# A decoder layer on one core: in each state-space chunk y's return stands one step earlier, the normalisation later, with a shorter Newton step

## The reference

```python
xz = x @ W_in.T;  x_ssm, z = split(xz)                 # state-space part, 512 channels, 16 states
x_ssm = silu(conv4(x_ssm) + conv_b)                    # causal, per channel
B, C, d = x_ssm @ W_x.T;  dt = softplus(d * W_dt + b_dt)
h[t] = exp(dt[t] * A) * h[t-1] + (x_ssm[t] * dt[t]) * B[t]
y[t] = sum_n h[t, :, n] * C[t, n] + x_ssm[t] * D
x = layernorm(x + (y * silu(z)) @ W_out.T)
x = layernorm(x + cross_attention(x, ctx))             # 16 heads, 154 context tokens
x = layernorm(x + moe(x))                              # 4 experts, the 2 best, weighted; moe adds its own x
```

## Time and profile before

| | us |
|---|---|
| median of 3 timed runs (1684.32 to 1684.8) | 1684.76 |
| the profiled execution | 1675.18 |
| its span | 1673.4 |
| granted TensorE clock, mean | 0.919 of full |

### The profile page before, as it was taken

How to read it: one execution, slowest core, us unless ns; L and a number is a source line. 1 busy time by engine, 2 the same in 40 slices (tenths; PEclk the granted TensorE clock), 3 DMA queues, 4 the chain that set the end, 5 groups by cost and what they waited for, 6 DMA issues and landing times. The chain is left out here.

```text
span 1673.4 us, 22601 instructions
## 1 busy us (share of the span) xinstructions
PE 1335.8 (80%) x7484; PEld 930.7 (56%) x7484; DVE 1465.3 (88%) x2698; ACT 1114.0 (67%) x2452; POOL 915.1 (55%) x663
## 2 busy tenths in 40 slices
PE   7687778788777877787886969988988898887880
PEld 5566556666656666565665644446445644462460
DVE  5999999999999999999999966697869786978578
ACT  5867887788788778878877524337633763375570
POOL 1778878877887788788778701102710271027015
PEclk9889899989989898998898989999999999999895
DMA  7201210220122022102102012100010000000000
GB/s 234 67 14 45 70 58 13 70 70 32 40 70 71 1 70 70 50 21 70 64 1 89 14 38 103 36 1 1 26 55 1 1 26 26 1 1 1 25 1 25
DMA packets 37927, 69.87 MB, mean 42 GB/s; under 512 B 3569, under 2 KB 31570, under 8 KB 33586
## 3 DMA queue, kind: packets, MB, share of 16 engines
q1 hardware_dynamic: 37810, 68.43, 12.0%
HBM read 59.77 MB, written 8.65 MB: 41 GB/s over the span
## 5 line engine op out<-in xcount | busy, mean ns | idle before, releaser
L900 POOL TENSOR_TENSOR state_c<-state,c_area 128x1024 f32<-128x1024 f32 x256 | 602.0, 2362 | 167.8 <-DVE state L970 148.9
L970 DVE TENSOR_TENSOR_SCAN state<-decay,ps 128x512 f32<-128x512 f32 x512 | 620.6, 1212 | 0.0
L686 ACT ACTIVATE decay<-step_area,negA 128x255 f32<-128x255 f32 x1024 | 432.6, 496 | 0.4 <-DVE step_area L1049 0.4
L945 DVE TENSOR_TENSOR ps<-step_area,ps 128x512 f32<-128x512 f32 x512 | 349.7, 683 | 8.0 <-PE ps L368 6.2
L384 PE MATMUL ps<-ident_sb,state_c 128*128 128x128 f32 x2048 | 293.3, 291 | 12.9 <-POOL state_c L900 11.9
L1578 POOL TENSOR_TENSOR big<-big,g_sb 128x1024 f32<-128x1024 f32 x29 | 79.4, 2739 | 406.6 <-ACT big L1467 404.9
L384 PEld LDWEIGHTS ps<-ident_sb,state_c 128*128 128x128 f32 x2048 | 253.5, 151 | 39.0 <-POOL state_c L900 21.5
L368 PE MATMUL ps<-parts,sel_bc_sb 96*128 96x256 bf16 x256 | 74.7, 292 | 102.7 <-DVE ps L961 80.2
L1391 PE MATMUL ps<-w_sb,weights 128*128 128x512 f32 x256 | 122.6, 615 | 0.0
L1426 PE MATMUL ps<-w_sb,hT 128*128 128x256 f32 x512 | 120.0, 388 | 2.4 <-ACT hT L1536 1.9
L1666 DVE BATCH_NORM_STATS2 stats<-big 128x6 f32<-128x256 f32 x256 | 88.4, 413 | 30.4 <-ACT big L1541 21.1
(11 more groups left out here) (211 smaller groups left out, 2357.9 us busy)
## 6 DMA issues: line engine op xcount, KB each, us to landing
c_area<-c_scratch SPq DMA_DIRECT2D x32, 1024.0 KB, 6.5
weights<-in_xT SPq DMA_DIRECT2D x16, 256.0 KB, 3.1
res<-in_x SPq DMA_DIRECT2D x16, 256.0 KB, 2.8
x_scratch<-res SPq DMA_DIRECT2D x16, 256.0 KB, 8.1
weights<-x_scratch SPq DMA_DIRECT2D x4, 1024.0 KB, 8.1
xa<-x_scratch SPq DMA_DIRECT2D x4, 1024.0 KB, 5.6
out_x<-acc SPq DMA_DIRECT2D x4, 1024.0 KB, 4.4
w_sb<-in_w SPq DMA_DIRECT2D x2, 1024.0 KB, 13.0
```

Source lines behind the costliest of these rows:

```text
L686: nc.scalar.activation(decay[:, n % RING, j, 1:], dt_sb[:, i[1] % 2, j, 1:], ACT.Exp, scale=negA[:, j * NS + n:j * NS + n + 1]).then_inc(s ...
L900: nc.gpsimd.tensor_tensor(state_c[:, n % RING, :, :], state[:, n % RING, :, :], c_bc[:, q, n, :].unsqueeze(1).to_broadcast([P, CT, TC]), A ...
L945: nc.vector.tensor_tensor(bu_ps[m % 3][:, :].rearrange("p (j n) -> p j n", j=2), u_sb[:, i[1] % 2, 2 * h:2 * h + 2, :], b_ps[n % 2][:, 0:T ...
L970: nc.vector.tensor_tensor_scan(state[:, n % RING, pair, :].rearrange("p j n -> p (j n)"), decay[:, n % RING, pair, :].rearrange("p j n -> ...
```

## The change

- PE (`turn`): `y_back`, `y_back`, `out_tile`, `out_tile` stand at steps 10, 11, 12 and 13 in every chunk; before it was 11 to 14, and 10 to 13 in the last alone.
- ACT: the copies of y stand at 13 and 14, the first sum at 15 of the same chunk, the second at step 0 of the next; the Silus at 9, not 10; `spreads` at 5, `guess` at 8, `normalise` at 13, where it is first in the list, ahead of `next_lead` and the first copy. `take_keys(0)` comes first in its list, and in the last chunk the keys', context's and queries' entries stand ahead of the others of the same step.
- GpSimd: `centre` stands at step 14 of the chunk in which the sums are taken, `variance` at 3, `newton` at 6.
- `variance` is one tensor_scalar operation (multiply, add) in place of two tensor_tensor ones, Newton's halving and subtraction likewise one; with `variance`'s that makes a step of six counted operations (`s_nw`), not seven. `centre` becomes a tensor_scalar. The constants' tile `coef` and its five fills are gone.

```diff
@@ PE, turn
                 if finish:
-                    early_by = 0 if prepare else 1
-                    work += [(11 - early_by, lambda: y_back(last, 0)), (12 - early_by, lambda: y_back(last, 1)),
-                             (13 - early_by, lambda: out_tile(last, 0)), (14 - early_by, lambda: out_tile(last, 1))]
+                    work += [(10, lambda: y_back(last, 0)), (11, lambda: y_back(last, 1)),
+                             (12, lambda: out_tile(last, 0)), (13, lambda: out_tile(last, 1))]
@@ ACT, turn
                 if settle:
-                    work += [(0, lambda: take_sum(old, 0)), (1, lambda: take_sum(old, 1)), (3, lambda: spreads(old)), (6, lambda: guess(old)),
-                             (9, lambda: normalise(old))]
+                    work += [(0, lambda: take_sum(old, 1)), (5, lambda: spreads(old)), (8, lambda: guess(old)),
+                             (13, lambda: normalise(old))]
                 if prepare:
                     work += [(3, lambda: take_xi(k, 0)), (4, lambda: take_xi(k, 1)), (5, lambda: take_conv(k, 0)), (7, lambda: take_conv(k, 1)), (8, lambda: take_z(k, 0)),
-                             (9, lambda: take_z(k, 1)), (10, lambda: silus(k)), (11, lambda: copies(k)),
+                             (9, lambda: take_z(k, 1)), (9, lambda: silus(k)), (11, lambda: copies(k)),
                              (12, lambda: terms(k, 0)), (12, lambda: terms(k, 1)), (12, lambda: terms(k, 2)),
                              (12, lambda: terms(k, 3)), (12, lambda: softplus(k)),
                              (13, lambda: next_lead(k))]
                 if finish:
-                    work += [(14, lambda: take_y_back(last, 0)), (15, lambda: take_y_back(last, 1))]
+                    work += [(13, lambda: take_y_back(last, 0)), (14, lambda: take_y_back(last, 1)), (15, lambda: take_sum(last, 0))]
                 if prepare:
                     work.append((15, lambda: first_decay(k)))
                 if i[1] == NCH - 2:
-                    work.append((13, lambda: take_keys(0)))
+                    work.insert(0, (13, lambda: take_keys(0)))
                 if i[1] == NCH - 1:
-                    work += [(4, lambda: take_keys(1)), ...
+                    early = [(4, lambda: take_keys(1)), ...
+                    work = early + work
@@ ACT, behind the turns
-            for t in range(CTT):
-                take_sum(shift(last, -1), t)
+            take_sum(shift(last, -1), 1)
@@ GpSimd, variance, centre, newton
-                nc.gpsimd.tensor_tensor(var[:, :], spread[:, :], per_dm, ALU.mult).then_inc(s_mv, 1)
-                pool.wait_ge(s_mv, at(k, 2, 2))
-                nc.gpsimd.tensor_tensor(var[:, :], var[:, :], eps, ALU.add).then_inc(s_nw, 1)
+                nc.gpsimd.tensor_scalar(var[:, :], spread[:, :], 1.0 / DM, LN_EPS, ALU.mult, ALU.add).then_inc(s_nw, 1)
-                nc.gpsimd.tensor_tensor(mean[:, :], total[:, :], minus_per_dm, ALU.mult).then_inc(s_mv, 1)
+                nc.gpsimd.tensor_scalar(mean[:, :], total[:, :], -1.0 / DM, None, ALU.mult).then_inc(s_mv, 1)
-                nc.gpsimd.tensor_tensor(newt[:, :], newt[:, :], half, ALU.mult).then_inc(s_nw, 1)
-                pool.wait_ge(s_nw, at(k, 7, 4))
-                nc.gpsimd.tensor_tensor(newt[:, :], one_half, newt[:, :], ALU.subtract).then_inc(s_nw, 1)
+                nc.gpsimd.tensor_scalar(newt[:, :], newt[:, :], -0.5, 1.5, ALU.mult, ALU.add).then_inc(s_nw, 1)
@@ GpSimd, turn
                 if settle:
-                    work += [(0, lambda: centre(old)), (2, lambda: variance(old)), (4, lambda: newton(old))]
+                    work += [(3, lambda: variance(old)), (6, lambda: newton(old))]
...
+                if finish:
+                    work.append((14, lambda: centre(shift(i, -1))))
```

More of the change, by code:

```diff
@@ L103, in mamba_block @@
         shift_sb = sb("shift_sb", [P, CTT])
-        coef = sb("coef", [P, 5, CTT])
         b_ps = [ps[:, k, :] for k in range(2)]
@@ L130, in mamba_block @@
         s_par = sem("s_par")
-        s_coef = sem("s_coef")
         s_in = sem("s_in")
@@ L653, in spreads @@
             def spreads(k):
-                act.wait_ge(s_mv, at(k, 2, 1))
+                act.wait_ge(s_mv, at(k, 1, 1))
                 for t in range(CTT):
@@ L662, in normalise @@
             def normalise(k):
-                act.wait_ge(s_nw, at(k, 7, 7))
+                act.wait_ge(s_nw, at(k, 6, 6))
                 for t in range(CTT):
@@ L670, in guess @@
             def guess(k):
-                act.wait_ge(s_nw, at(k, 7, 1))
+                act.wait_ge(s_nw, at(k, 6, 1))
                 nc.scalar.activation(lnv[:, :], var[:, :], ACT.Ln).then_inc(s_ln, 1)
@@ L749, in turn @@
                 if i[1] == NCH - 2:
-                    work.append((13, lambda: take_keys(0)))
+                    work.insert(0, (13, lambda: take_keys(0)))
                 if i[1] == NCH - 1:
-                    work += [(4, lambda: take_keys(1)), (5, lambda: take_context(0)), (6, lambda: take_context(1)),
+                    early = [(4, lambda: take_keys(1)), (5, lambda: take_context(0)), (6, lambda: take_context(1)),
                              (6, lambda: take_context(2)), (7, lambda: take_context(3)), (7, lambda: take_values(False)),
                              (8, lambda: take_values(True))]
-                    work += [(9 + v, lambda v=v: take_query(v)) for v in range(G + 1)]
-                    work += [(15, lambda: spare_keys())]
+                    early += [(9 + v, lambda v=v: take_query(v)) for v in range(G + 1)]
+                    early += [(15, lambda: spare_keys())]
+                    work = early + work
                 for n in range(NS):
@@ L868, in newton @@
                 nc.gpsimd.tensor_tensor(newt[:, :], rstd[:, :], rstd[:, :], ALU.mult).then_inc(s_nw, 1)
-                pool.wait_ge(s_nw, at(k, 7, 2))
+                pool.wait_ge(s_nw, at(k, 6, 2))
                 nc.gpsimd.tensor_tensor(newt[:, :], newt[:, :], var[:, :], ALU.mult).then_inc(s_nw, 1)
-                pool.wait_ge(s_nw, at(k, 7, 3))
-                nc.gpsimd.tensor_tensor(newt[:, :], newt[:, :], half, ALU.mult).then_inc(s_nw, 1)
-                pool.wait_ge(s_nw, at(k, 7, 4))
-                nc.gpsimd.tensor_tensor(newt[:, :], one_half, newt[:, :], ALU.subtract).then_inc(s_nw, 1)
-                pool.wait_ge(s_nw, at(k, 7, 5))
+                pool.wait_ge(s_nw, at(k, 6, 3))
+                nc.gpsimd.tensor_scalar(newt[:, :], newt[:, :], -0.5, 1.5, ALU.mult, ALU.add).then_inc(s_nw, 1)
+                pool.wait_ge(s_nw, at(k, 6, 4))
                 nc.gpsimd.tensor_tensor(rstd[:, :], rstd[:, :], newt[:, :], ALU.mult).then_inc(s_nw, 1)
-                pool.wait_ge(s_nw, at(k, 7, 6))
+                pool.wait_ge(s_nw, at(k, 6, 5))
                 nc.gpsimd.tensor_tensor(shift_sb[:, :], mean[:, :], rstd[:, :], ALU.mult).then_inc(s_nw, 1)
@@ L907, in _ @@
             nc.gpsimd.memset(decay[:, :, :, 0], 0.0).then_inc(s_zero, 1)
-            for c, value in enumerate((0.5, 1.5, 1.0 / DM, LN_EPS, -1.0 / DM)):
-                nc.gpsimd.memset(coef[:, c, :], value).then_inc(s_coef, 1)
-            half, one_half, per_dm, eps, minus_per_dm = (coef[:, c, :] for c in range(5))
             pool.sem_inc(s_sum, RING)
@@ L913, in _ @@
             nc.gpsimd.memset(ones[:, :], 1.0).then_inc(s_ones, 1)
-            pool.wait_ge(s_coef, 5)
             first, last = (None, 0), (None, NCH - 1)
@@ L920, in _ @@
             for k in (shift(last, -1), last):
-                centre(k)
+                if k == last:
+                    centre(k)
                 variance(k)
```

## The result

The changed kernel takes 1698.2 us (median of 4 runs, 1697.07 to 1699.82); the kernel before, in 4 runs beside it, 1684.54 (1682.09 to 1684.8). The ratio is 1.0085, with a 95% interval of 1.0068 to 1.0103: slower, 2.8 us under the 1701 forecast. The profiled execution took 1699.82 us (span 1698.0, clock 0.919), 24.6 more than the profiled one of before. Of the two differences, 13.7 timed and 24.6 profiled, the larger one rests on a single reading of before, and the smaller on four; the first experiment shows how far such readings scatter. One later run of before, 1754.45 us at a granted clock of 0.799, is left out of every ratio.

The account below looks back on a forecast made before the run. VectorE, busy 892.1 of 900 us in the chunks, was taken as the bound. New idle 22.9 us (twelve chunks x 1.5, plus 2.2, 2.2, 0.5) less 6.3 gives +16.6 on the 1684.76 median: 1701.4 us, range 1684 to 1717.

Parts of the forecast that it names:

- the 1701 forecast: Whole kernel: net +16.6 us added to the timed median of 1684.76 gives 1701.4 us; chance 0.72.
- The mechanism: Chunk ends: second transposition ahead of row 14, output tile ahead of row 15; PE waits for y's copy, rows come late.
- X: Price of an ordinary chunk in VectorE idle time near rows 14 and 15: 1.5 us, taken between 0.1 and 2.95.
- The half-clock end: Upper end of X: all PE work from transposition to row 15 at half clock, row 15 2.95 us late.
- The full-clock end: Lower end of X: all at full clock, second copy sets the output tile's start, row 15 0.1 us late.
- a share of 2.2 for five chunks: Extra 2.2 us in all for chunks 4, 8, 12 (no VectorE carry additions) and those after 4 and 12 (ACT late).
- Chunk 14: `keys(0)` and `y_back` share PE's step 10; transposition waits for ACT's two key copies, row 13 2.2 us late.
- Chunk 1: Has no `normalise`; cost 0 to 1.4 us, taken as 0.5.
- The last chunk: Key copies no longer behind the mean and a pair of squares; two row-product stalls go, gain 2.4 us (0 to 2.7).
- The sum: VectorE idle time: 22.9 us new, 6.3 off (boundary and last-chunk waits), net +16.6 us.
- Faster: Rival: VectorE's waits go and none comes, with y's copy at 653 instead of 655; 1679.6 us, chance 0.13.
- Half clock throughout: Rival: every ordinary chunk (2 to 13) pays 2.95 us, last chunk's 2.4 not gained; +37, 1722 us, chance 0.06.

Follow-up runs that it names:

- the first experiment: The kernel before, unchanged, profiled a second time: 1678.44 us, 3.3 more than its first profiled run.
- the first two edits: PE's four steps put back in the changed kernel: 1673.74 us, ratio to before 0.9951; PE's steps alone moved in the kernel before: 1722.61 us, 1.0236.
- the eight zero products: Changed kernel plus eight PE products with a tile of zeros, added into y's bank ahead of the second transposition's wait: 1683.04 us, ratio to before 0.9994.
- `normalise` last: Changed kernel with ACT's `normalise(old)` still at step 13 but last in the list, behind the first copy of y: 1683.77 us, ratio to before 1.0002.
- the two experiments before the last: Kernel before with only ACT's copies and first sum moved, keys first: 1698.14 us; PE's-steps-back kernel with Silus at 10, `normalise` at 9: 1713.11 us.

## Why the prediction was right, and where it was not

*The mechanism was right.* PE's steps carry the loss, as the first two edits show; it comes through what is queued behind the second transposition, and through the clock. The copy of y was to come 1.2 us earlier against row 14: it starts 1.81 us ahead of it (669.63, 671.44) where it was 0.56: 1.25, of which 0.1 is row 14's own delay (against row 13's product it is 1.15). PE's wait: "about 4", 4.02. The idle time ahead of `make_bu` is 28.7 us where 25 were named, and ACT's waits for GpSimd's mean are gone. The two waits a chunk came in chunks 3, 4, 8 and 12 alone: at row 14 the others wait 0.2 us or less, where I had 0.35. The clock was to fall ahead of the transposition; it does so in the odd chunks 3 to 13 and in 14, and just behind its start in the other ones from 2 to 12. I hadn't thought of that case, and in the ordinary chunks it is the cheap one.

*X, the price of an ordinary chunk*, was 1.5 between 0.1 and 2.95. It is no number in between but two: 0.8 to 1.05 in chunks 2, 6 and 10, where the clock comes back inside the output product well before its end, and 1.9 to 2.1 in 5, 7, 9, 11 and 13, where it is at half nearly to the end (chunk 3, where the copy is 0.9 us later than in these, has 2.67). That 1.5 lies between the two is why the middle served; the average of these eight is 1.6. The half-clock end was 0.9 too high: between transposition and row 15's multiplication I had 7.6 us, chunk 11 shows 6.83 (729.42 to 736.25), most of it because I doubled the full rate of output tile and input to 4.3, which took 3.70. The full-clock end, 0.1, agrees with the eight zero products, where these rows wait nowhere. The Trainium skill ("TensorE: Matmul & The Clock Gate", "HAM oscillation — how this bites in real kernels") has each pass with a long wait restart at the low clock; the trace agrees in that chunks 2 to 14 all have such a stretch around their wait of 3.2 to 4.0 us, and differs in chunk 1, where the clock stays at full through 3.04 us. By it alone X was to be near 2.95; measured is 0.8 to 2.1.

*Chunks 4, 8 and 12 were mis-sized.* I had them at 1.5 plus a share of 2.2 for five chunks, 1.9; they cost 2.4 each. ACT's copy is there no earlier against VectorE than before, 3.1 us behind row 13's product. The cause stands at the start of the chunk, PE, after, then before:

```profile
512.82 1.39 PE L382 MATMUL ps<-ident_sb,state_c 128*128 128x128 f32 x8 [1.95 <-DVE yg L924]
514.01 5.04 PE L303 MATMUL ps<-weights 128*128 128x256 f32 x16
```

```profile
503.29 3.62 PE L305 MATMUL ps<-weights 128*128 128x256 f32 x16
```

With PE's steps back, in the same chunk:

```profile
501.79 3.62 PE L303 MATMUL ps<-weights 128*128 128x256 f32 x16
```

PE waits for VectorE's gating of y, its clock falls, and the convolution takes 5.04 us instead of 3.62; ACT waits for it 5.59 us and is late up to the copy. I had looked for low-clock stretches only around the copy of y. With PE's four steps back and all else as in after, the convolution stays at full clock in this chunk and the copy stands 1.8 us behind row 13's product in all three, so the lateness comes with PE's early steps. By what way is open: with the eight products of zeros the copy is late in chunks 4 and 8 (3.1 and 2.8 us) and not in 12 (1.8), with `normalise` last in 12 alone (2.1, against 0.8).

*Chunk 14*: 2.58 us at row 13, forecast 2.2, by the mechanism named; it went away with the one step given back. *Chunk 1*: nothing at rows 14 and 15, forecast 0.5. *The last chunk* gained 0.9 us, forecast 2.4: rows 6 and 7 still wait 0.93 each where the earlier trace rows has 1.81 and 0.93. The sum was +16.6 on VectorE's idle time and the trace shows +20.7: +2.3 in chunks 2 to 13, +0.4 in 14, +1.5 in the last; the rest are small ones both ways. That this gave 1701 against 1698 is partly luck, two misses that offset: between the profiled executions the time grew by 24.6 us, 8.0 more than the sum, and the median to which I added the sum lay 9.6 above the profiled time of before.

*The gain was in the sum, its cause was not.* The sum takes 6.3 us off, waits at chunk boundaries and in the last chunk. With PE's steps back the rest of the change gives 0.4 to 0.5%, 6 to 8 us, and the idle time falls from 8.0 (11.2 in the second execution) to 4.5 us. But I had set down ACT's waits for GpSimd's mean as ACT's idle time alone. Behind them PE waits too, at `in_proj`; the waits view of before and of the kernel with PE's steps back:

```profile
PE ps L288 <- ACT weights L586: 29.7, 14, 2.9
```

```profile
PE ps L286 <- ACT weights L584: 5.2, 4, 1.7
```

In such a wait PE's clock can fall and a row come late, as row 5 did in the first experiment; over 30 to 930 us half clock is on for 126 us against 181. I read ACT's idle time for its length, not for what PE does meanwhile. That the gain comes by this way fits these figures, but no run takes the waits for the mean away alone; taken in pieces, the change without its PE part turns into a loss (the two experiments before the last).

*The rivals.* "Faster" needed the copy of y 2 us earlier than I counted; one microsecond more brings no difference (`normalise` last). "Half clock throughout" is nearly what chunks 5, 7, 9, 11 and 13 do, at 1.9 to 2.1 us and not 2.95. That PE's steps alone in the kernel before took 1722.6, this rival's figure, is chance: there the copy of y is 1.2 to 1.6 us later as well.

## What to carry to other kernels

On an engine that takes its work in order, a step moved ahead is moved ahead of everything queued behind its wait: here it was row 14's and row 15's product. The first of the four steps was harmless outside chunk 14, the other three together were not. What follows, though no run tries it in this form: move the producer (ACT's copy) first and the waiting steps only as far as it went. The version to use is the change without its PE part: 1673.7 and 1674.7 us, 0.4 to 0.5% faster than before.

## What the runs showed of the hardware

Equal work behind equal waits (4.02 and 4.03 us) ran at half clock for 3.4 us in chunk 10 and for 5.9 in chunk 11 of after, which more than doubles the price of the wait (0.77 and 1.98 us). Waits of 3.04 us passed without a fall of the clock in chunk 1 of after and in chunks 5, 6 and 13 with `normalise` last, and with a fall in others of that kernel. Products of zeros hold the clock up as others do: it is at full behind them where it was 0.50. Before's first 12 runs lie 18 us apart (1672 to 1690), the 9 of the kernel with PE's steps back, beside them, 4, and 10 later ones of the same kernel 11; why is open. The attention and expert part behind the last chunk, the same code in all kernels, took between 711.2 and 721.9 us, and 717.5 and 721.4 in two executions of one kernel.
